# Two adjacency pieces loaded and widened during the expert slots, the ranks of a block taken three steps earlier, and no zero matmuls in front

## The chip, the cores and the metric

One Trainium2 chip, one core. The metric is the device time of one execution in microseconds (us), the median of several runs.

## The reference, cut to what matters

A two-layer graph network (each node averages the features of its neighbours over 100,000 edges), a layer norm, and then three layers in which every node's averaged state goes to two of eight experts. Weak experts are one matrix with a relu, strong ones two matrices with a relu between.

```python
def _sage_conv(x, src, dst, W_l, b_l, W_r):
    summed = jax.ops.segment_sum(x[src], dst, num_segments=N_NODES)
    cnt = jax.ops.segment_sum(jnp.ones((src.shape[0],), x.dtype), dst, num_segments=N_NODES)
    return (summed / jnp.maximum(cnt, 1.0)[:, None]) @ W_l + b_l + x @ W_r
...
h = x @ W_in + b_in
for l in range(3):
    agg = segment_sum(h[src], dst, num_segments=N) / deg
    logits = concatenate([h, agg], axis=-1) @ router_W[l] + router_b[l]
    vals, idx = top_k(logits, 2); gates = softmax(vals, axis=-1)
    weak = relu(einsum('nh,ehf->nef', agg, weak_W[l]) + weak_b[l])
    sh = relu(einsum('nh,ehf->nef', agg, strong_W1[l]) + strong_b1[l])
    strong = einsum('nef,efh->neh', sh, strong_W2[l]) + strong_b2[l]
    moe = einsum('ne,neh->nh', gate_dense, concatenate([weak, strong], axis=1))
    h = h + sigmoid(h @ conf_W[l] + conf_b[l]) * moe
return h @ W_out + b_out
```

There are 3125 nodes, padded to 25 tiles of 128; the state h has 256 columns, the inner layer of a strong expert 512.

## The kernel before, in words

Every engine has its own instruction stream, and the streams meet at semaphores; nothing reorders the work, so its order is the order of the code.

**Prelude.** TensorE first issues 110 zero matmuls (L1388). Then four chunks of key look-ups (chunk m: four passes of L1397 and 8 times L1399, then 8 times L1401), each behind the comparison that VectorE writes for it (L710). VectorE's tables follow from them, and then a long loop builds the adjacency matrix by one-hot matmuls (L1424 to L1431; VectorE's one-hots L754).

**Aggregation.** The adjacency is stored in DRAM as 25 pieces (NB = 5 blocks of destination nodes b, NK = 5 groups of source nodes k). A piece is 128x3200 bf16, 800 KB, and holds SK = 5 steps s of 128x640. Passes p = 0 to 2 (`gather`, L1484) multiply bf16 pieces. Beside the matmuls of a block, TensorE does small work of the block before at places (k, s): in pass 2 the turning and projection at PLACES, and `ranks` (L1549, L1551), which counts how many rows before each row chose the same expert, at (3, 4). `ranks` waits for the choice of the block before (VectorE L966, semaphore a_sel); VectorE's `positions` (L922) waits for `ranks`. After block 3 of pass 2, VectorE also fills the table of the first EARLY = 12 slots (`table_counts`, `table_experts`, `table_places`) before it goes on to block 4 (`block_of_nodes`, L813); TensorE waits for that block with L1455.

Passes p = 3 and 4 are the experts' aggregations (`aggregate`, L1571). The state is kept as two fp32r halves: ScalarE copies the high half (`high_half`, L1328) out of the loaded new states `h_new`, and VectorE subtracts to get the low half (`low_half`, L1110). This goes in eight units u of tiles (UNITS: 1, 1, 1, 2, 5, 5, 5, 5 tiles). Pieces come as bf16 into the three buffers of `ring3` (`expert_piece`, L504) and are widened to fp32r by ScalarE (`widen`, L1317), in turns into `wide_a` and `wide_b`. Block 0 waits for its widened piece (e_conv) and at each step s for the low half of that tile's unit (c_lo).

**Slots.** Each of passes 2, 3 and 4 ends with SLOTS = 32 slots of 256 rows of one expert. SyncE loads the rows of slot j (L530) into one of three buffers once slot j - 3 is finished. TensorE turns them (L1646), multiplies by the first weights (L1657, `slot_hidden`) and the second (L1668, `slot_output`); ScalarE copies the turned rows (L1338) and takes the relu of four parts (L1341); VectorE adds the bias and scales (L1103, L1105); GpSimd adds the rows into h_rows in DRAM by an indirect DMA (L659). In TensorE's stream `slot_turn(j + 1)`, `slot_output(j)`, `slot_hidden(j + 1)` follow each other.

**From slots to the next aggregation.** When the last indirect DMA has landed, SyncE loads the new states u = 0 to 7 (`new_states_in`, L537), with pieces 0, 1, 2 of block 0 behind u = 3, 4, 5. `ring3` and `wide_b` lie on the same memory as the slots' buffers; `wide_a` and the high and low halves don't. There are two such changeovers, p = 2 to 3 and p = 3 to 4.

## Time and profile before

| | us |
|---|---|
| median of 3 runs | 2048.9 (2045.55 to 2051.56) |
| the profiled execution | 2050.06 |
| its span, first to last instruction | 2048.1 |
| TensorE busy | 1787.7 (87%) |
| VectorE busy | 892.3 (44%) |
| ScalarE busy | 829.3 (40%) |
| GpSimd busy | 618.4 (30%) |

The mean granted TensorE clock is 0.898 of full speed. The page of the profile has six parts: busy time, the span in slices, the DMA queues, the chain of work that ended last, groups of instructions with the idle time before them, and the DMA issues. A timeline row gives the start in us, the busy time, engine, line, operation and tiles, the count of merged instructions and, in brackets, how long the engine was idle before it and what released it.

### The profile page before, as it was taken

To read this page: it belongs to the slowest core of one execution; us is meant where nothing else is said; L and a number is where in the kernel's file an instruction comes from. 1 tells how busy PE (TensorE), PEld (TensorE's weight loads), DVE (VectorE), ACT (ScalarE), POOL (GpSimd) and SP (SyncE) were. 2 spreads that over 40 slices of the span, in tenths; PEclk is the share of its full clock that TensorE was granted. 3 is DMA by queue.
4 is the path that set the end of the run, shared out by engine and by line. 5 is a ranking of instruction groups with operands and counts; after the bars stand their busy time and mean duration, and the time that the engine had idled before them with its cause. 6 is when DMAs were issued, how large, how long until landed. Compare 5 with 4: busy or idle time off the path is not lost.

```text
span 2048.1 us, 30902 instructions
## 1 busy us (share of the span) xinstructions
PE 1787.7 (87%) x9855; PEld 1380.5 (67%) x9858; DVE 892.3 (44%) x2593; ACT 829.3 (40%) x1388; POOL 618.4 (30%) x593
## 2 busy tenths in 40 slices
PE   9756666689999997999969998999969998999974
PEld 4545555455666664888858877888858877888864
DVE  6679999744344435433321113533321113533324
ACT  6256666534322222333336563333336563333321
POOL 1234444300000033544430231544430231544430
PEclk8766666599999998999989998999989998999986
DMA  6970000224567772444457551444457551444441
GB/s 143 340 265 0 0 0 0 85 98 162 205 195 235 260 280 100 87 75 73 72 116 271 188 188 43 90 74 74 72 125 260 188 188 43 90 74 74 72 116 51
DMA packets 162537, 259.55 MB, mean 127 GB/s; under 512 B 27776, under 2 KB 136043, under 8 KB 162424
## 3 DMA queue, kind: packets, MB, share of 16 engines
q1 hardware_dynamic: 125960, 206.09, 31.3%
q0 software_dynamic: 36464, 51.98, 14.5%
q8 instruction: 68, 1.11, 0.2%
q14 instruction: 45, 0.37, 0.1%
HBM read 149.08 MB, written 108.94 MB: 126 GB/s over the span
## 4 chain that ended last, share of the span: by engine, by line
PE 76%; DVE 12%; issue 5%; ACT 3%; DMA 2%; DVEq 1%; SPq 1%; POOL 0%; ACTq 0%; POOLq 0%
PE psum L1657 17%; PE psum L1668 16%; PE psum L1484 14%; PE psum L1571 13%; DVE arena L754 7%; PE psum L1623 2%; PE psum L1464 2%; PE psum L1646 2%; PE psum L1431 2%; PE psum L1399 2%; PE psum L1429 1%; PE psum L1690 1%; PE psum L1617 1%; ACT wide_b L1317 1%; ACT wide_a L1317 1%
## 5 line engine op out<-in xcount | busy, mean ns | idle before, releaser
L659 POOL DMA_INDIRECT h_rows<-arena,idx x192 | 313.7, 1634 | 420.1 <-DVE arena L1105 386.8
L1341 ACT ACTIVATE arena<-psum,b1c 128x256 f32<-128x256 f32 x384 | 182.2, 475 | 465.6 <-PE psum L1657 465.5
L1657 PE MATMUL psum<-arena 128*128 128x256 f32 x1536 | 360.2, 388 | 7.2 <-ACT arena L1338 7.2
L1668 PE MATMUL psum<-arena 128*128 x1536 | 347.4, 379 | 0.0
L1657 PEld LDWEIGHTS psum<-arena 128*128 128x128 f32 x1536 | 280.1, 192 | 72.0 <-ACT arena L1341 20.0
L1484 PE MATMUL psum<-arena 128*128 128x384 bf16 (+1 forms) x1875 | 318.2, 327 | 0.5 <-ACT arena L1233 0.2
L1668 PEld LDWEIGHTS psum<-arena 128*128 128x128 f32 x1536 | 284.6, 190 | 34.8
L754 DVE TENSOR_TENSOR arena<-arena 125x1200 bf16<-125x1200 bf16 (+1 forms) x300 | 282.0, 1006 | 23.6 <-PE psum L1431 23.0
L634 POOL DMA_INDIRECT xs_d<-arena,pos x150 | 146.6, 978 | 404.8 <-DVEq L936 362.7
L1484 PEld LDWEIGHTS psum<-arena 128*128 128x128 bf16 x1875 | 181.9, 98 | 126.6 <-ACT arena L1236 3.3
L1103 DVE TENSOR_TENSOR arena<-psum,arena 128x256 f32<-128x256 f32 x192 | 80.9, 421 | 381.9 <-PE psum L1668 380.8
L594 POOL TENSOR_TENSOR arena<-arena 128x100 bf16 x200 | 136.1, 680 | 248.4 <-ACT arena L1194 244.8
L1571 PE MATMUL psum<-halves,wide_b 128*128 128x512 f32 x625 | 161.3, 402 | 19.4 <-ACT wide_b L1317 18.4
L1571 PE MATMUL psum<-halves,wide_a 128*128 128x512 f32 x625 | 161.2, 402 | 17.9 <-ACT wide_a L1317 16.8
L1196 ACT CAST arena<-psum 128x800 f32 x200 | 165.6, 828 | 0.2 <-issue 0.2
L1571 PEld LDWEIGHTS psum<-halves,wide_b 128*128 128x128 f32 x625 | 114.2, 190 | 42.2 <-issue 21.0
L1571 PEld LDWEIGHTS psum<-halves,wide_a 128*128 128x128 f32 x625 | 114.2, 190 | 40.7 <-issue 19.4
L1431 PE MATMUL psum<-arena 125*128 125x100 bf16 x1200 | 139.6, 270 | 0.0
L1431 PEld LDWEIGHTS psum<-arena 125*128 125x128 bf16 x1200 | 122.7, 134 | 25.0
L1424 PE MATMUL psum<-arena 128*128 128x2 bf16 x200 | 37.4, 187 | 110.9 <-DVE arena L754 95.5
L1429 PE MATMUL psum<-arena 125*128 125x200 bf16 (+1 forms) x400 | 108.4, 368 | 0.0
L1424 PEld LDWEIGHTS psum<-arena 128*128 128x128 bf16 x200 | 21.6, 108 | 126.7 <-issue 81.2
(252 smaller groups left out, 1772.8 us busy)
## 6 DMA issues: line engine op xcount, KB each, us to landing
arena<-adj_d SPq DMA_DIRECT2D x50, 800.0 KB, 4.4
ring<-adj_d SPq DMA_DIRECT2D x50, 800.0 KB, 4.4
xs_d<-zrow SPq DMA_DIRECT2D x8, 3432.0 KB, 27.3
arena<-xs_d SPq DMA_DIRECT2D x96, 264.0 KB, 2.8
adj_d<-arena SPq DMA_DIRECT2D x25, 800.0 KB, 4.1
h_rows<-zrow SPq DMA_DIRECT2D x1, 8192.0 KB, 39.3
h_new<-h_rows SPq DMA_DIRECT2D x12, 640.0 KB, 8.3
arena<-h_rows SPq DMA_DIRECT2D x10, 640.0 KB, 6.3
```

Source lines behind the costliest of these rows:

```text
L594: pool.tensor_tensor(a, first_w[:, u % 8], a, ALU.add).then_inc(s_first, 1)
L634: pool.indirect_dma_start(xs_d, bass.IndirectOffsetOnAxis(ap=pos[:, b % 2, k, t:t + 1], axis=0), pay_of(p, b)[:, k, t], None).then_inc(a_s ...
L659: pool.indirect_dma_start(h_rows, bass.IndirectOffsetOnAxis(ap=idx[:, j % 2, h:h + 1], axis=0), ybuf[:, j % 2, h], None, compute_op=ALU.ad ...
L754: v.tensor_tensor(oh, every, keys.rearrange("p (n o z) -> p n o z", z=2, o=1).broadcast_to(shape), ALU.is_equal).then_inc(ready, 1)
L1196: act.copy(adj[:, bass.ds(off[u] + WC, G * WC)].rearrange("p (b n) -> p b n", b=2), banks[:, :, WC:WC + GA]).then_inc(s_wide, 1)
L1341: act.activation(hid[:, j % 2, f], psum[:, 5 + f % 2, 0:M], ACT.Relu, bias=b1c[:, bass.ds(at_b1[j % LOAD] + f, 1)]).then_inc(b_hidf, 1)
L1429: pe.matmul(bank[:, 0:cols], oh1[:, q, n, :, z % 2], ohe[:, q % 2, g, 0:cols, z], start=(z == 0), stop=False, skip_group_check=True)
L1431: mm = pe.matmul(bank[:, bass.ds(rel[(q % 2 * k + g) * (G - NST) + z - NST], WC)], oh1[:, q, n, :, z % 2], oh2[:, q, (g * (G - NST) + z - ...
L1484: return pe.matmul(psum[:, t, 0:width], ring[:, k, s, t * P:(t + 1) * P], features[p][:, k * SK + s, 0:width], start=(k == 0 and s == 0), ...
L1571: return pe.matmul(psum[:, t, :], adj32[piece_no(p, b, k) % 2][:, s, t * P:(t + 1) * P], halves[:, k * SK + s].rearrange("p k f -> p (k f) ...
L1657: mm = pe.matmul(psum[:, 5 + f % 2, 0:M], w1s[:, j % 2, f // 2, kt, f % 2 * P:(f % 2 + 1) * P], xsT[:, j % 2, kt], start=(kt == 0), stop=( ...
L1668: mm = pe.matmul(psum[:, h, 0:H], hid[:, j % 2, f, h * P:(h + 1) * P], w1f[:, bass.ds(at_w2 + f * H, H)], start=(f == 0), stop=(f == FT - 1))
```

## The change

- Pieces 0 and 1 of block 0 of the next pass get a buffer `early` of their own, on the memory of the last 6400 bf16 columns of `halves` (tiles 18 to 24). SyncE loads both at slot EARLY = 12, when the scatters that read `pay_b` are done.
- ScalarE widens piece 0 in five parts of 128x640, one behind the relus of each of slots 22 to 26. Piece 1 goes into `wide_b` in five parts between the high halves: two behind u = 2, one behind u = 3, two behind u = 4. TensorE waits for it part by part (e_second).
- Pieces 2, 3 and 4 of block 0 go through `ring3`: loaded behind u = 4, 5 and 6 of the new states. Piece 2 is widened behind u = 5; pieces 3 and 4 in the stream of block 0.
- `ranks` of pass 2 goes from (3, 4) to (3, 1).
- The 110 zero matmuls are gone.

```diff
+        early = carve([2, SK, BN], BF16)
...
+            def early_piece(p, k):
+                sp.dma_start(early[:, k].rearrange("p s n -> p (s n)"), adj_d[:, k]).then_inc(e_early[k], 16)
+
             def expert_piece(p, b, k):
-                m = piece_no(p, b, k)
-                if b == 0 and k == 0:
-                    for g in range(2):
-                        sp.wait_ge(b_sc[g], 32 * SLOTS // 2 * (p - 2))
-                if m > 2:
-                    sp.wait_ge(e_conv, m - 2)
-                sp.dma_start(ring3[:, m % 3].rearrange("p s n -> p (s n)"), adj_d[:, b * NK + k]).then_inc(e_in[m % 3], 16)
+                r = ring_no(p, b, k)
+                if b:
+                    sp.wait_ge(e_conv, piece_no(p, b, k) - 2)
+                sp.dma_start(ring3[:, r % 3].rearrange("p s n -> p (s n)"), adj_d[:, b * NK + k]).then_inc(e_in[r % 3], 16)
...
                         sp.wait_ge(b_tab, 2 * (p - 2) + 2)
+                        if p < 4:
+                            for k in range(2):
+                                early_piece(p + 1, k)
...
                     new_states_in(p, u)
-                    if 3 <= u < 6 and p < 4:
-                        expert_piece(p + 1, 0, u - 3)
+                    if 4 <= u < 7 and p < 4:
+                        expert_piece(p + 1, 0, u - 2)
...
+            def widen_early(p, k, s):
+                if s == 0:
+                    act.wait_ge(e_early[k], 16 * (p - 2))
+                ins = act.copy(adj32[k][:, s], early[:, k, s])
+                if s == SK - 1:
+                    ins.then_inc(e_conv, 1)
+                elif k:
+                    ins.then_inc(e_second, 1)
...
+                    if p < 4 and SLOTS - 2 * SK <= j < SLOTS - SK:
+                        widen_early(p + 1, 0, j - (SLOTS - 2 * SK))
...
+                        if u == 6:
+                            act.wait_ge(e_second, (SK - 1) * (p - 1))
+                            act.wait_ge(e_conv, piece_no(p + 1, 0, 1) + 1)
                         high_half(p, u)
-                        if u == 3 or u == 4:
-                            widen(p + 1, 0, u - 3)
+                        if u == 5:
+                            widen(p + 1, 0, 2)
+                        for s in {2: (0, 1), 3: (2,), 4: (3, 4)}.get(u, ()):
+                            widen_early(p + 1, 1, s)
...
-            for _ in range(110):
-                pe.matmul(psum[:, 7, :], zeros_b[:, :], ones_b[:, :], start=True, stop=True)
...
-                        if n > 3 * NB - 1 and (k, s) == (3, 4):
+                        if n > 3 * NB - 1 and (k, s) == (3, 1):
                             ranks(2, n - 3 * NB)
...
                         for s in range(SK):
+                            if b == 0 and k == 1 and s < SK - 1:
+                                pe.wait_ge(e_second, (SK - 1) * (p - 3) + s + 1)
+                            elif b == 0 and k == 1:
+                                pe.wait_ge(e_conv, piece_no(p, b, k) + 1)
```

The new lines stand 10 to 28 lines lower in the changed kernel, so the same instruction has another line number there. ScalarE at the changeover from pass 2 to pass 3, before (behind the last relu of the slots, L1341; L1328 are the high halves, L1317 the widenings; ring_51 is `ring3`):

```order
L1341 ACTIVATE arena<-psum,b1c 128x256
L1328 CAST halves<-h_new 128x256 x3
L1328 CAST halves<-h_new 128x2x256
L1317 CAST wide_a<-ring_51 128x3200
L1328 CAST halves<-h_new 128x5x256
L1317 CAST wide_b<-ring_51 128x3200
L1328 CAST halves<-h_new 128x5x256 x3
```

and of the change (L1359 is the relu, L1346 the high half, L1331 a part from `early`, which lies in the arena, L1326 a widening from `ring3`):

```order
L1359 ACTIVATE arena<-psum,b1c 128x256
L1346 CAST halves<-h_new 128x256 x3
L1331 CAST wide_b<-arena 128x640 x2
L1346 CAST halves<-h_new 128x2x256
L1331 CAST wide_b<-arena 128x640
L1346 CAST halves<-h_new 128x5x256
L1331 CAST wide_b<-arena 128x640 x2
L1346 CAST halves<-h_new 128x5x256
L1326 CAST wide_a<-ring_51 128x3200
L1346 CAST halves<-h_new 128x5x256 x2
```

The widening of piece 0 is gone from here, and that of piece 1 is cut in five.

SyncE's DMAs at the same place, before (L537 new states, L504 pieces):

```order
L537 DMA h_new<-h_rows 128x256 x3
L537 DMA h_new<-h_rows 128x512
L504 DMA ring_51<-adj_d 128x3200
L537 DMA h_new<-h_rows 128x1280
L504 DMA ring_51<-adj_d 128x3200
L537 DMA h_new<-h_rows 128x1280
L504 DMA ring_51<-adj_d 128x3200
L537 DMA h_new<-h_rows 128x1280 x2
L504 DMA ring_51<-adj_d 128x3200 x2
```

and of the change (L547, L511):

```order
L547 DMA h_new<-h_rows 128x256 x3
L547 DMA h_new<-h_rows 128x512
L547 DMA h_new<-h_rows 128x1280
L511 DMA ring_51<-adj_d 128x3200
L547 DMA h_new<-h_rows 128x1280
L511 DMA ring_51<-adj_d 128x3200
L547 DMA h_new<-h_rows 128x1280
L511 DMA ring_51<-adj_d 128x3200
L547 DMA h_new<-h_rows 128x1280
```

Two pieces fewer are loaded here, and the unit u = 4 stands where the first piece stood.

TensorE in the last quarter of block 4 of pass 2, before (L1484 the aggregation, L1549 the first matmul of the ranks, L1551 its last, L1455 the turning of block 4):

```order
L1484 MATMUL psum<-arena 128x384 x50
L1549 MATMUL psum<-sel,tri 128x48
...
L1551 MATMUL psum<-sel,ones_s 128x8
L1484 MATMUL psum<-arena 128x384 x25
L1455 MATMUL psum<-ident,arena 128x128 x4
```

and of the change (L1507, L1572, L1574, L1478):

```order
L1507 MATMUL psum<-arena 128x384 x35
L1572 MATMUL psum<-sel,tri 128x48
...
L1574 MATMUL psum<-sel,ones_s 128x8
L1507 MATMUL psum<-arena 128x384 x40
L1478 MATMUL psum<-ident,arena 128x128 x4
```

The ranks stand 15 matmuls sooner.

## Rows read from the trace of the kernel before

**Rows 1.** Page, parts 1 and 4: TensorE's busy time, the last chain by engine.

```profile
PE 1787.7 (87%) x9855; PEld 1380.5 (67%) x9858; DVE 892.3 (44%) x2593; ACT 829.3 (40%) x1388; POOL 618.4 (30%) x593
...
PE 76%; DVE 12%; issue 5%; ACT 3%; DMA 2%; DVEq 1%; SPq 1%; POOL 0%; ACTq 0%; POOLq 0%
```

**Rows 2.** Timeline of the changeover from pass 2 to pass 3.

```profile
1064.03 1.77 SPq L537 DMA_DIRECT2D h_new<-h_rows  x4
1065.89 0.38 SPq L504 DMA_DIRECT2D ring<-adj_d  x1
...
1066.60 1.31 DVE L1110 TENSOR_TENSOR halves<-h_new,halves 128x256 fp32r<-128x256 f32 x3 [8.35 <-ACT halves L1328]
...
1068.56 0.62 ACT L1328 CAST halves<-h_new 128x512 fp32r<-128x512 f32 x1 [1.10 <-DMA h_new<-h_rows]
...
1070.62 2.86 ACT L1317 CAST wide_a<-ring 128x3200 fp32r<-128x3200 bf16 x1 [1.44 <-DMA ring<-adj_d]
...
1073.72 7.37 PE L1571 MATMUL psum<-halves,wide_a 128*128 128x512 f32 x25 [16.79 <-ACT wide_a L1317]
...
1080.85 1.27 ACT L1328 CAST halves<-h_new 128x1280 fp32r<-128x1280 f32 x1 [0.32 <-DMA h_new<-h_rows]
1080.93 5.83 PE L1571 MATMUL psum<-halves,wide_b 128*128 128x512 f32 x25
```

**Rows 3.** Timeline of the changeover from pass 3 to pass 4.

```profile
1525.63 0.86 DVE L1110 TENSOR_TENSOR halves<-h_new,halves 128x256 fp32r<-128x256 f32 x2 [8.25 <-ACT halves L1328]
...
1534.42 7.42 PE L1571 MATMUL psum<-halves,wide_b 128*128 128x512 f32 x25 [18.35 <-ACT wide_b L1317]
```

**Rows 4.** Timeline of ScalarE between two slots of pass 2.

```profile
1046.21 0.47 ACT L1341 ACTIVATE arena<-psum,b1c 128x256 f32<-128x256 f32 x1 [0.39 <-PE psum L1657]
...
1046.58 0.58 ACT L1338 COPY arena<-psum 128x512 f32<-128x512 f32 x1
...
1050.96 0.47 ACT L1341 ACTIVATE arena<-psum,b1c 128x256 f32<-128x256 f32 x1 [3.80 <-PE psum L1657]
```

**Rows 5.** Groups by line: ScalarE's copies of 128x640 and 128x3200, mean ns.

```profile
L1317 ACT CAST wide_a<-ring 128x3200 fp32r<-128x3200 bf16 x25 | 71.6, 2864 | 49.7 <-PE psum L1571 48.3 <-DMA ring<-adj_d 1.4
...
L408 ACT COPY arena<-arena 128x640 bf16<-128x640 bf16 x45 | 29.0, 721 | 5.4 <-PE psum L1484 5.3
```

**Rows 6.** Page, part 6: count, KB each, us from issue to landing.

```profile
arena<-adj_d SPq DMA_DIRECT2D x50, 800.0 KB, 4.4
...
arena<-xs_d SPq DMA_DIRECT2D x96, 264.0 KB, 2.8
```

**Rows 7.** Timeline around the ranks of block 3 of pass 2.

```profile
782.54 8.30 PE L1484 MATMUL psum<-arena 128*128 128x384 bf16 x50
...
786.02 0.20 DVE L966 TENSOR_TENSOR sel<-arena 128x40 bf16<-128x40 f32 x1
...
791.09 0.20 DVE L922 TENSOR_TENSOR arena<-psum,nxt 128x40 f32<-128x40 f32 x1 [4.14 <-PE psum L1551]
...
803.29 1.09 PE L1455 MATMUL psum<-ident,arena 128*128 128x128 f32 x4 [8.21 <-DVEq L825]
```

**Rows 8.** Timeline of TensorE in the prelude.

```profile
2.15 25.32 PE L1388 MATMUL psum<-arena 128*128 128x512 bf16 x108 [2.15 <-POOL arena L577]
30.31 0.38 PE L1397 MATMUL psum<-arena 1*125 1x400 bf16 x1 [2.84 <-DVE arena L710]
...
44.74 0.59 PE L1397 MATMUL psum<-arena 1*125 1x400 bf16 x1
...
60.31 0.38 PE L1397 MATMUL psum<-arena 1*125 1x400 bf16 x1
...
76.01 1.52 PE L1401 MATMUL psum<-arena 100*125 100x400 bf16 x8
```

**Rows 9.** Windows of 2 us: span, busy by engine, granted clock, DMA share, GB/s.

```profile
32.00:34.00 2.00, 2.00 (x8) 1.25 (x7) 0.95 (x3) 2.00 (x1) 0.00 (x0) 0.58 0.42 3
...
58.00:60.00 2.00, 2.00 (x8) 1.41 (x7) 0.00 (x0) 0.00 (x0) 0.00 (x0) 0.59 1.09 341
```

More of the change, by code:

```diff
@@ L322, in build @@
         c_hi = sem("high_halves"); c_lo = sem("low_halves")
+        e_early = [sem(f"early_piece_in_{k}") for k in range(2)]; e_second = sem("second_piece_widened")
         e_in = [sem(f"expert_piece_in_{k}") for k in range(3)]
@@ L385, in piece_no, with ring_no @@
             return (p - 3) * NB * NK + b * NK + k
+        def ring_no(p, b, k):
+            return (p - 3) * (NB * NK - 2) + b * NK + k - 2
         def unit_of(t):
@@ L1308, in widen @@
             def widen(p, b, k):
-                m = piece_no(p, b, k)
-                act.wait_ge(e_in[m % 3], 16 * (m // 3 + 1))
-                if m > 1:
-                    n, last = divmod(m - 2, NK)
-                    if last < NK - 1:
-                        act.wait_ge(e_used, (NK - 1) * n + last + 1)
-                    else:
-                        act.wait_ge(a_sum, sums_before(NB + n + 1))
-                act.copy(adj32[m % 2][:, :, :], ring3[:, m % 3]).then_inc(e_conv, 1)
+                m, r = piece_no(p, b, k), ring_no(p, b, k)
+                act.wait_ge(e_in[r % 3], 16 * (r // 3 + 1))
+                n, last = divmod(m - 2, NK)
+                if last < NK - 1:
+                    act.wait_ge(e_used, (NK - 1) * n + last + 1)
+                else:
+                    act.wait_ge(a_sum, sums_before(NB + n + 1))
+                act.copy(adj32[(b * NK + k) % 2][:, :, :], ring3[:, r % 3]).then_inc(e_conv, 1)
+            def widen_early(p, k, s):
[6 more added lines that the diff above has]
+                    ins.then_inc(e_second, 1)
             def low_sums(p, b):
@@ L1360, in _ @@
                         else:
-                            for k in range(2, NK):
+                            for k in range(3, NK):
                                 widen(p, b, k)
```

10 lines of the change are left out of this document (6 added, 4 removed).

## The prediction

> **What bounds the kernel now.** I read the page first: TensorE is busy 87% of the span and carries 76% of the chain that ended last [rows 1]. So a saved microsecond counts where TensorE stands still and somebody else is late. The table of waits, longest first, then gives TensorE's long single waits, and only three of them are touched here: the two changeovers from the slots to the next aggregation [rows 2, 3] and the wait for block 4 of pass 2 [rows 7]. Last I read the prelude, where zero matmuls are taken out [rows 8, 9]. In each timeline the reader should look at the bracket behind TensorE's row: how long it was idle, and who ended that.
>
> In the first changeover TensorE was idle for 16.79 us, until ScalarE had widened piece 0. The order of events is: new states issued at 1064.03; piece 0 issued behind four of them at 1065.89; the first low halves at 1066.60; piece 0 landed only at 1070.62, and its widening took 2.86 us; TensorE at 1073.72 [rows 2]. The second one is alike, 18.35 us, with the first low halves at 1525.63 and TensorE at 1534.42 [rows 3]. So the wait that ends last there is the load and the widening of the piece, and the next behind it is the low half of the first tile.
>
> **Term 1, the changeovers: -14.5 us.** Piece 0 is ready before the slots end. What is late next is the low half of unit 0. In the first changeover three low halves take 1.31 us, 0.44 each, so the first is done at 1066.60 + 0.44 = 1067.04. TensorE followed the widening by 1073.72 - (1070.62 + 2.86) = 0.24 us, so it starts at 1067.28: 6.4 us sooner [rows 2]. In the second: 1525.63 + 0.86/2 + 0.24 = 1526.30 against 1534.42: 8.1 us [rows 3]. The loads of u = 0 to 3 and all before them keep their order, so nothing moves that start.
>
> The start alone is no gain if TensorE stalls behind it. Step by step, in the first changeover:
> - Piece 0 takes TensorE 7.37 us in five steps of 1.5, so step 3 comes at 1071.7. It wants the low half of u = 3. ScalarE now puts two parts of piece 1 ahead of that unit's high half. A copy of 128x640 takes 721 ns [rows 5] (bf16 to bf16, the nearest row; a fifth of the whole widening, 2864/5 = 573, is the lower bound, and I take 721). So the high half moves from 1068.56 [rows 2] to about 1069.5 and the low half ends near 1070.9. In time, with 0.8 us to spare.
> - Piece 1 is wanted at 1067.28 + 7.37 = 1074.65. Its last parts come behind the high half of u = 4, and this unit is now loaded where piece 0 stood. It is smaller (640 KB against 800), so it lands by 1070.6 [rows 2]. High half about 1.3 us and two parts 1.4 us: piece 1 is ready near 1073.5. The new memory for both pieces is written during the slots.
> - Piece 2 is wanted 5.83 us after piece 1 [rows 2], at 1080.5. Its buffer is free when piece 0 is used up, at 1074.65; with 2.86 us of widening it is ready near 1078.
> - Piece 3 is wanted at 1086.3, and may be widened from 1080.5 on. ScalarE has to take the high half of u = 7 first. Before, the last unit landed by 1080.85 [rows 2], behind seven units and three pieces; now it stands behind seven units and three pieces as well, so at the same time. Its high half ends at 1082.1 and piece 3 is ready at 1085.0, with 1.3 us to spare. This is the thinnest place; I take no wait, and keep 0 to 4 us per changeover (the widening and the high half both on the path) for the range.
>
> **Term 2, the restart: +1.0 us.** The first 25 matmuls after the idle time took 7.37 us and the next 25 took 5.83 [rows 2]: after the standstill TensorE runs at the lower of its two clock levels and rises within the first piece. This costs 1.5 us already. How soon the clock rises after an earlier start isn't shown. From zero (as before) to another 1.5 us each; I take 0.5 for each changeover.
>
> **Term 3, the slots: 0, cover named.** Five of the 32 slots of two passes get a ScalarE copy of 0.72 us behind the last relu. It delays the copy of the next turned rows, which starts at 1046.58 and takes 0.58; the first user is the relu at 1050.96, behind 3.80 us of idle time of ScalarE [rows 4]. 0.72 of 3.80 fits, and TensorE meanwhile has the 16 matmuls of `slot_output`. If the cover were gone, it would cost 10 x 0.72 = 7.2 us. The two early pieces are issued on SyncE's queue ahead of the rows of slot 12, but behind those of slot 11, so they have a whole slot, 7.4 us, before the rows of slot 12 are due to be issued; a piece takes 4.4 us to land, the rows 2.8 (medians) [rows 6]. If the loads overlap fully, those rows land some 4 us late, and they are needed a slot after their issue. Cost 0, at most 2 x 4.4 = 9 us.
>
> The GpSimd queue is touched only through the DMA engines: its indirect adds run on while 1.6 MB go by. The Trainium skill, page "DMA: Bandwidth & Descriptors", section "Queues, rings and completion order", says that each DMA engine takes turns between the queues that have work for it. By that rule a slot's add would land some us later once per pass; two slots may pass before VectorE's buffer is needed, so the sum would stay the same.
>
> **Term 4, the ranks: -2.5 us.** VectorE had nothing to do for 4.14 us until `ranks` came, at 791.09. From there it runs without a gap through positions, slot table and block 4, and TensorE waits 8.21 us for that, until 803.29 [rows 7]. The ranks now come 15 matmuls sooner: 15 x 8.30/50 = 2.5 us, at 788.2. The choice that they need is there at 786.02 + 0.20 [rows 7], 2 us before, so TensorE doesn't wait for it. VectorE's chain and TensorE's start move by the full 2.5. What is late next is TensorE's own aggregation, which ended 8.2 us sooner; there is room. The three other blocks of the pass have the same pattern with nobody waiting behind the ranks: 0.
>
> **Term 5, the zero matmuls: +1.8 us.** They end at 27.5, and VectorE's comparison lets the first real ones go only at 30.31 [rows 8]: none of the 25.3 us is on the path. What they leave is the clock. The granted clock falls within the window from 32 us and rises again within that from 58 us [rows 9]. At full clock a chunk takes (77.53 - 60.31)/2 = 8.6 us; the second, nearly all at half clock, took 15.57, and with its last 0.7 us at half clock 16.2; the first took 14.43, as it began at full clock [rows 8]. Without the zero matmuls the first is at half clock too: 16.2 - 14.4 = +1.8 us, all on TensorE's path, since it has no idle time between chunks. Floor: the clock may rise at the end of the first chunk instead of the second: 15.6 + 3 x 8.6 = 41.4 against 47.2 before, -5.8. Ceiling: a chunk later, 2 x 16.2 + 15.6 + 8.6 = 56.6, +9.4.
>
> The Trainium skill, page "TensorE: Matmul & The Clock Gate", section "Why this matters for your kernels", advises to warm TensorE up first and warns that a pause gives the clock back. Its first half speaks against this edit, its second says that the warm-up was largely wasted, as the 2.8 us pause stood behind it; rows 8 and 9 show both, and the sum goes by them.
>
> **Sum.** -14.5 + 1.0 + 0 - 2.5 + 1.8 = -14.2 us on the profiled execution, 2050.06 to 2035.9. The median of before is 2048.9, 1.2 us under that execution, so I forecast 2048.9 - 14.2 = **2034.7 us**. Nothing between these places waits for a transfer with a fixed date, so savings pass on to the end.
>
> **Rivals.**
> - *The clock rises a chunk sooner in the prelude* (-5.8 instead of +1.8): 2027.1. For it: the last matmuls of the first chunk are of the same kind as those in which it rose. Against: it did not rise there before. 0.17.
> - *It rises a chunk later* (+9.4): 2042.3. 0.08.
> - *Pieces 2 to 4 or the parts of piece 1 come late*, and TensorE stands still again 3 to 4 us in each changeover: 2034.7 + 7 = about 2042. For it: five parts on ScalarE in a chain where everything waits for everything. Against: the step list above. 0.15.
> - *The slots are lengthened* by the copies or by the 1.6 MB ahead of slot 12: +7.2 to +9, 2042 to 2044. Against it: 3.80 us of idle time [rows 4]. 0.06.
> - *The changeovers do not shorten*, since the low half isn't the next but something not seen, such as the memory of piece 1: 2034.7 + 14.5 - 1 = 2048.2, no difference. 0.03.
> - *Slower*: without the zero matmuls the clock stays at half level through all four chunks of the prelude: 4 x 16.2 = 64.8 against 47.2, +17.6 in place of +1.8: 2050.5. It decides from the point where the prelude loses over 1.8 + 14.2 = 16.0 us, and loses more than 0.3% only if the one-hot loop behind it slows as well. Against: the clock rose in matmuls that stay. 0.02.
>
> The forecast itself has 0.49. The range: 2027.1 stands at the lower end and 2042 to 2043 at the upper, so **2027 to 2043**; it leaves out the two last rivals and a tail at each side. A difference of under 0.3%, 6.1 us, can't be told from none with this kernel. So faster is everything under 2042.8: 0.91; within 0.3%: 0.07; slower: 0.02.
>
> **What the profile of the changed kernel would show.** TensorE's wait at each changeover about 10.3 us, ended by VectorE's low half, not by ScalarE's widening; no second wait of over 1 us in the two pieces behind it. Slots 22 to 26 as long as the others, 7.4 us. The wait for block 4 down from 8.2 to about 5.8. No L1388, the first chunk of the prelude 16.2 us, and the end of the last chunk at 79.3. What would make the prediction wrong: another place of the rise in the prelude; a wait of TensorE for piece 2 or 3; VectorE's chain behind the ranks held by another wait.

## The result, and the profile after

The changed kernel takes 2038.7 us, the median of 5 runs (2032.5 to 2041.0), against 2048.9 us before, also of 5 runs (2045.6 to 2056.2). The ratio is 0.9948 (0.9931 to 0.9965): 10.2 us or 0.5% faster. The forecast was 2034.7 us, a gain of 14.2. The profiled execution took 2040.89 us with a span of 2039.1, so it stands 9.2 us below the profiled execution of before. The same kernel, run again later beside its own runs of before, gave 2035.0 us against 2047.4, ratio 0.9936 (0.9916 to 0.9957). Ratios leave out runs that lie over 1.5% above the fastest run of the same kernel, while medians in us hold all runs; this matters only for the second group of experiments below.

The page gives TensorE 15.7 us less busy time than [rows 1], in 108 fewer matmul records, which are the zero matmuls (25.3 us); the rest of TensorE's work is longer by some 10 us, at the lower clock. TensorE's share of the last chain is the same. Part 1 and part 4 of the page of after:

```profile
PE 1772.0 (87%) x9747; PEld 1376.1 (67%) x9748; DVE 892.9 (44%) x2593; ACT 829.7 (41%) x1404; POOL 619.0 (30%) x593
...
PE 76%; DVE 12%; issue 5%; ACT 3%; DMA 2%; DVEq 1%; SPq 1%; POOL 0%; ACTq 0%; POOLq 0%
```

**The changeovers.** The table of TensorE's waits of after (waiter and releaser, us in total, times, longest) has both of them in one row, ended by VectorE's low half:

```profile
PE psum L1594 <- DVE halves L1120: 20.4, 2, 10.2
```

The timeline of the first one (start, duration, engine and line, tiles, count, idle time before and who ended it) answers to [rows 2]; its last row is the start of the second, which answers to [rows 3]:

```profile
1068.76 8.71 PE L1594 MATMUL psum<-halves,wide_a 128*128 128x512 f32 x25 [10.18 <-DVE halves L1120]
1077.31 5.83 PE L1594 MATMUL psum<-halves,wide_b 128*128 128x512 f32 x25
...
1088.64 5.83 PE L1594 MATMUL psum<-halves,wide_b 128*128 128x512 f32 x25
...
1072.91 1.35 ACT L1331 CAST wide_b<-arena 128x640 fp32r<-128x640 bf16 x2
...
1077.56 2.87 ACT L1326 CAST wide_a<-ring 128x3200 fp32r<-128x3200 bf16 x1 [0.44 <-PE psum L1594]
...
1082.94 1.26 ACT L1346 CAST halves<-h_new 128x1280 fp32r<-128x1280 f32 x1 [1.35 <-DMA h_new<-h_rows]
1084.11 2.87 ACT L1326 CAST wide_b<-ring 128x3200 fp32r<-128x3200 bf16 x1
...
1522.81 8.68 PE L1594 MATMUL psum<-halves,wide_a 128*128 128x512 f32 x25 [10.19 <-DVE halves L1120]
```

The waits fell from 16.79 to 10.18 us and from 18.35 to 10.19. Behind the start TensorE has no gap. Piece 3, the thinnest place, was ready at 1084.11 + 2.87 = 1086.98 and wanted at 1088.64, so 1.7 us were left where 1.3 had been worked out. Most of that margin came from the slow first piece: with 7.37 us in place of 8.71, piece 3 would have been wanted 1.3 us sooner. In e2_early_only, whose first piece took 7.52 us at the second changeover, TensorE did wait 0.48 us for piece 3. But the first 25 matmuls now take 8.71 and 8.68 us, where they took 7.37 and 7.42. The granted clock says why. Windows of 2 us from the new start (span, busy time by engine, granted clock, DMA share, GB/s) stay at 0.50, the lower level of 1.2 GHz, until the fourth:

```profile
1072.00:1074.00 2.00, 2.00 (x6) 1.54 (x5) 0.96 (x1) 2.00 (x3) 0.00 (x0) 0.50 0.98 408
1074.00:1076.00 2.00, 2.00 (x9) 1.64 (x8) 0.53 (x1) 0.41 (x2) 0.00 (x0) 0.82 1.04 431
```

**The ranks.** The timeline answers to [rows 7]: the wait for block 4 fell from 8.21 to 5.78 us.

```profile
793.20 0.19 PE L1572 MATMUL psum<-sel,tri 128*128 128x48 bf16 x1
...
805.82 0.45 PE L1478 MATMUL psum<-ident,arena 128*128 128x128 f32 x1 [5.78 <-DVEq L835]
```

**The prelude.** The timeline of TensorE answers to [rows 8], with the start of each of the four chunks, the same eight matmuls ahead of the rise and behind it, and the last matmuls:

```profile
30.80 0.56 PE L1420 MATMUL psum<-arena 1*125 1x400 bf16 x1 [30.80 <-DVE arena L720]
...
46.95 0.59 PE L1420 MATMUL psum<-arena 1*125 1x400 bf16 x1
47.47 2.93 PE L1422 MATMUL psum<-arena 100*125 100x400 bf16 x8
...
63.12 0.59 PE L1420 MATMUL psum<-arena 1*125 1x400 bf16 x1
...
76.49 2.27 PE L1424 MATMUL psum<-arena 100*125 100x400 bf16 x8
78.69 0.38 PE L1420 MATMUL psum<-arena 1*125 1x400 bf16 x1
79.00 1.57 PE L1422 MATMUL psum<-arena 100*125 100x400 bf16 x8
...
85.82 1.52 PE L1424 MATMUL psum<-arena 100*125 100x400 bf16 x8
```

The first two chunks take 16.2 us each, and the third 15.6: the clock rose only at its end, near 78 us, a chunk later than before. The prelude ends at 87.3 us where it ended at 77.5.

Here the level has to be read from the durations (eight equal matmuls take 2.93 us or 1.57 us). A window of after, in the form of [rows 9], shows a granted clock of 1.00 in the middle of the slow stretch:

```profile
60.00:62.00 2.00, 2.00 (x8) 1.38 (x7) 0.00 (x0) 0.00 (x0) 0.00 (x0) 1.00 1.08 340
```

The column reads 1.00 through the slow part of the prelude in every execution without matmuls ahead of it. So the mean granted clock of such a kernel (0.907 for after) is too high, and can't be held against the 0.898 of before.

Putting the profiled executions side by side at five places (us; the end of the prelude, the end of the one-hot loop at VectorE's first lay-out copy, TensorE's start on block 4 of pass 2, its start on pass 3 and on pass 4):

| | prelude | loop | block 4 | pass 3 | pass 4 | span |
|---|---|---|---|---|---|---|
| before | 77.5 | 393.3 | 803.3 | 1073.7 | 1534.4 | 2048.1 |
| after | 87.3 | 399.9 | 805.8 | 1068.8 | 1522.8 | 2039.1 |
| difference | +9.8 | +6.6 | +2.5 | -5.0 | -11.6 | -9.0 |

The pieces of that -9.0 are: waits at the changeovers -14.8, restart +2.6 (1.34 and 1.26), ranks -2.4, prelude +9.8, and -3.2 that the one-hot loop gives back. Another -1.4 is one stretch near 462 to 472 us in which before had a granted clock of 0.83 and after 1.00. That makes -9.4, and +0.4 is left over.

### The profile page after: what moved, and what is told of

Read it like the earlier page. It is cut to its first block, busy times and chain, and to the rows that moved or that the text cites. A ratio compares the mean times of both kernels' runs of the same rounds, so it can differ in the third digit from the quotient of the medians.

```text
span 2039.1 us, 30707 instructions
## 1 busy us (share of the span) xinstructions
PE 1772.0 (87%) x9747; PEld 1376.1 (67%) x9748; DVE 892.9 (44%) x2593; ACT 829.7 (41%) x1404; POOL 619.0 (30%) x593
## 3 DMA queue, kind: packets, MB, share of 16 engines
q0 software_dynamic: 36464, 51.98, 14.5%
## 4 chain that ended last, share of the span: by engine, by line
PE 76%; DVE 12%; issue 5%; ACT 3%; DMA 2%; DVEq 1%; SPq 1%; POOL 0%; ACTq 0%; POOLq 0%
PE psum L1685 17%; PE psum L1696 16%; PE psum L1507 14%; PE psum L1594 13%; DVE arena L764 7%; PE psum L1651 2%; PE psum L1487 2%; PE psum L1674 2%; PE psum L1422 2%; PE psum L1454 2%; PE psum L1452 1%; PE psum L1645 1%; PE psum L1718 1%; DVEq L764 1%; PE psum L1478 1%
## 5 line engine op out<-in xcount | busy, mean ns | idle before, releaser
L1359 ACT ACTIVATE arena<-psum,b1c 128x256 f32<-128x256 f32 x384 | 181.8, 473 | 462.5 <-PE psum L1685 462.5
L1507 PE MATMUL psum<-arena 128*128 128x384 bf16 (+1 forms) x1875 | 316.9, 326 | 0.5 <-ACT arena L1243 0.2
L1507 PEld LDWEIGHTS psum<-arena 128*128 128x128 bf16 x1875 | 181.5, 98 | 125.7 <-ACT arena L1246 3.2
L1594 PE MATMUL psum<-halves,wide_a 128*128 128x512 f32 x650 | 171.3, 409 | 21.5 <-DVE halves L1120 20.4
L1594 PE MATMUL psum<-halves,wide_b 128*128 128x512 f32 x600 | 153.8, 400 | 1.1 <-issue 1.1
L1594 PEld LDWEIGHTS psum<-halves,wide_a 128*128 128x128 f32 x650 | 121.8, 195 | 46.6 <-issue 23.4
L1594 PEld LDWEIGHTS psum<-halves,wide_b 128*128 128x128 f32 x600 | 108.5, 188 | 22.1 <-issue 2.2
```

What stands on the lines that cost most here:

```text
L1359: act.activation(hid[:, j % 2, f], psum[:, 5 + f % 2, 0:M], ACT.Relu, bias=b1c[:, bass.ds(at_b1[j % LOAD] + f, 1)]).then_inc(b_hidf, 1)
L1507: return pe.matmul(psum[:, t, 0:width], ring[:, k, s, t * P:(t + 1) * P], features[p][:, k * SK + s, 0:width], start=(k == 0 and s == 0), ...
L1594: return pe.matmul(psum[:, t, :], adj32[(b * NK + k) % 2][:, s, t * P:(t + 1) * P], halves[:, k * SK + s].rearrange("p k f -> p (k f)"), s ...
```

## The experiments

Three theories were to be told apart. **A:** the early pieces bring 14 us or more, and the clock of the prelude is a matter of chance that the zero matmuls don't decide. **B:** the zero matmuls were of use, and taking them out costs the missing 4 us (or the 9.8 us of the profile). **C:** the copies and loads among the slots cost something that the changeovers' gain hides. The experiments ran in three groups, and each group had its own chip and its own runs of before. The chip of the second group is slower as a whole; the last section comes back to it.

**The parts, one at a time**

e1_zeros_back is the changed kernel with the zero matmuls back:

```diff
@@ tensor, ahead of the prelude
             pe.wait_ge(s_const, 4)
+            for _ in range(110):
+                pe.matmul(psum[:, 7, :], zeros_b[:, :], ones_b[:, :], start=True, stop=True)
```

> The changed kernel with the 110 zero matmuls back in front. Theory A (the zero matmuls only keep the first 2 us of the prelude at full clock; in which chunk the clock rises is chance): the first chunk is 1.8 us shorter than in the changed kernel, the median 1 to 2 us lower, 2037, and the chunk of the rise differs from run to run in both. Theory B (without the zero matmuls the clock rises a chunk later as a rule): the prelude's last look-up matmul ends near 77.5 us instead of 87.3, and the median is 5 to 7 us lower, about 2033.

e2_early_only also puts the ranks back, so only the early pieces are left of the change:

```diff
-                        if n > 3 * NB - 1 and (k, s) == (3, 1):
+                        if n > 3 * NB - 1 and (k, s) == (3, 4):
```

> Kernel before with the early pieces alone (zero matmuls kept, ranks at (3, 4)). Theory: both changeovers shrink as in the changed kernel, 6.6 and 8.2 us to TensorE's first matmul, less 1.3 us each because the clock stays low longer behind it: 12.2 us together, 2036.7. The slots keep their 7.4 us. Rival (the copies of ScalarE or the loads at slot 12 lengthen the slots): under 10 us gained, with slots 12 to 14 or 22 to 26 longer.

e3_ranks_only is the kernel before with only that line changed the other way:

```diff
-                        if n > 3 * NB - 1 and (k, s) == (3, 4):
+                        if n > 3 * NB - 1 and (k, s) == (3, 1):
```

> Kernel before with the ranks at (3, 1) alone. Theory: TensorE's wait for block 4 of pass 2 goes from 8.2 to 5.7 us, and the slots begin 2.5 to 3 us sooner; about 2046. Rival (VectorE's chain is held by another wait): wait stays over 7 us, no difference.

e4_no_zeros_only is the kernel before without the 110 zero matmuls:

```diff
-            for _ in range(110):
-                pe.matmul(psum[:, 7, :], zeros_b[:, :], ones_b[:, :], start=True, stop=True)
```

> Kernel before without the zero matmuls, nothing else. Theory A: first chunk of the prelude 16.2 us instead of 14.4, median 1 to 2 us higher, about 2050.5. Theory B (the clock rises a chunk later as a rule): prelude ends 9 to 10 us later, of which some 3 come back in the one-hot loop behind it; about 2055.

Against 2049.1 us for before (23 runs), in the same group:

| | median us (runs) | ratio, interval | prelude ends | changeover waits |
|---|---|---|---|---|
| e1_zeros_back | 2033.1 (6) | 0.9934, 0.9911 to 0.9956 | 70.0 | 10.14, 10.06 |
| e2_early_only | 2035.1 (6) | 0.9930, 0.9914 to 0.9947 | 71.0 | 10.20, 10.06 |
| e3_ranks_only | 2047.9 (12) | 0.9997, 0.9981 to 1.0013 | 79.2 | 17.22, 17.33 |
| e4_no_zeros_only | 2047.4 (12) | 0.9990, 0.9975 to 1.0005 | 79.7 | 16.82, 16.91 |

The early pieces alone bring 14 us, at least what the whole change brings, so they are the change. The ranks alone cut their wait to the same length as in the changed kernel, as the timeline of e3_ranks_only shows:

```profile
787.59 0.19 PE L1549 MATMUL psum<-sel,tri 128*128 128x48 bf16 x1
...
800.21 1.09 PE L1455 MATMUL psum<-ident,arena 128*128 128x128 f32 x4 [5.78 <-DVEq L825]
```

In the time of the whole kernel those 2.4 us can't be told from nothing. Taking the zero matmuls out alone costs nothing that can be measured: 1.7 us less, with 5 us less and 1 us more as ends. That speaks against B, which expected 2055 us. Theory A had expected 1 to 2 us more, and that isn't seen either. Its 12 runs lie in groups, at 2043 to 2044, 2046 to 2049 and 2052 to 2055 us, as they might if the rise fell into one chunk or another; the one with a trace (2052.2 us) is of the slowest group, with the rise in the second chunk. The timelines show the rise itself. In e4_no_zeros_only it comes near 61 us, in the second chunk, as in before. In e1_zeros_back, which has the zero matmuls, it comes within the first:

```profile
30.76 0.38 PE L1422 MATMUL psum<-arena 1*125 1x400 bf16 x1 [2.92 <-DVE arena L720]
...
39.45 2.93 PE L1424 MATMUL psum<-arena 100*125 100x400 bf16 x8
42.17 2.09 PE L1426 MATMUL psum<-arena 100*125 100x400 bf16 x8
44.19 0.38 PE L1422 MATMUL psum<-arena 1*125 1x400 bf16 x1
```

Over all profiled executions, the chunk in which the clock rose was:

| | first | second | third |
|---|---|---|---|
| with 110 zero matmuls (before, e1, e2, e3) | 2 | 2 | 0 |
| without (after, e4, e7, e8, e9, e12, e13) | 3 | 3 | 1 |

So neither kernel fixes it. The changed kernel, unaltered, ended its prelude at 87.3, 73.7 and 79.1 us (after, e9, e13), with the rise in the third, first and second chunk. In every one of these executions TensorE is busy without a gap through the chunks at the lower level, and once the clock rises the rest of the prelude is at the upper one. In all eleven the rise falls within the last eight matmuls of a chunk, those of the ones matrix (L1401 of before), which then take 2.0 to 2.7 us where they take 2.87 at the lower level and 1.52 at the upper. So the rise isn't free to come anywhere; what is special there, and what picks the chunk, is not shown.

**Clock kept up: a bridge and fillers**

e5_zeros_bridge lets the zero matmuls last until the prelude's first real one, with no pause:

```diff
             pe.wait_ge(s_const, 4)
+            for _ in range(126):
+                pe.matmul(psum[:, 7, :], zeros_b[:, :], ones_b[:, :], start=True, stop=True)
```

> The changed kernel with 126 zero matmuls in front, 16 more than before had, so that they last until the first comparison is ready (about 30.9 us) and TensorE has no pause ahead of the look-ups. If the pause is what took the clock away, the whole prelude stays at full clock: four chunks of 8.6 us, last look-up at 65.5 us instead of 87.3 in the changed kernel (70 to 71 with 110 zero matmuls in two runs with an early rise), median 2028 to 2032. If the look-up matmuls themselves don't keep the clock, it falls within the first chunk all the same and the time is that with 110, about 2033.

The clock never fell. The chunks took 8.6 us each, and the prelude ended at 66.4 us. The 16 extra matmuls were a few too many, and held up the first real one to 32.0 us, about 1 us. The time was 2119.5 us (12 runs), ratio 0.9960 (0.9921 to 0.9999), against 2128.9 for before and 2125.0 for e9_changed_again, the changed kernel as it is on that chip, with ratio 0.9968. From these two ratios no gain of the bridge can be told.

e8_fillers puts matmuls of the identity into the wait at each changeover:

```diff
                     pe.wait_ge(b_yt, 2 * SLOTS * (p - 2))
+                    for _ in range(72):
+                        pe.matmul(psum[:, 3, 0:P], ident[:, :], ident[:, :], start=True, stop=True)
```

> The changed kernel with 72 matmuls of the identity with itself in each of the two changeovers, into a bank nobody reads, while TensorE waits for the first low half. They last about 8 of its 10.2 us. If the low clock is what makes the first piece slow (8.7 us for 25 matmuls against 5.8), the first piece takes 5.8 and each changeover gains 2.9 us, 5.8 together, about 2033 against the changed kernel. Rival: the fillers hold up the first real matmul, or the first piece is slow because of its waits for low halves step by step; no gain or a loss of some us.

The edit was mis-sized. A matmul of fp32 by fp32 has two records of 0.11 us each, so 72 of them are 144 records and last 16.3 us, past the low half that was being waited for. Timeline of e8_fillers:

```profile
1059.89 16.32 PE L1604 MATMUL psum<-ident 128*128 128x128 f32 x144 [1.08 <-DVE arena L1113]
1075.96 5.95 PE L1594 MATMUL psum<-halves,wide_a 128*128 128x512 f32 x25
```

The start came some 6 us too late. Its time, 2128.9 us (6 runs, 2096.9 to 2139.4; ratio 0.9894, 0.9801 to 0.9987), is spread too widely to say anything. The second row does: the first 25 matmuls took 5.95 us and not 8.6. So the whole slow restart is the clock, and it goes when TensorE is kept busy. How much it costs without fillers doesn't follow the length of the wait. The first 25 matmuls behind each changeover, first and second, took (us): with the long waits of before 7.37 and 7.42 (before), 7.29 and 7.36 (e4), but 8.43 and 8.29 (e3); with waits of 10 us 8.71 and 8.68 (after), 8.70 and 8.74 (e1), 8.70 and 8.64 (e13), 8.57 and 8.39 (e9), 8.20 and 8.69 (e7), but 7.28 and 7.52 (e2), 7.31 and 7.55 (e12), and 7.26 and 8.29 (e5). In e5 it differs within one execution, between two waits of 10.1 us. The unaltered changed kernel, though, has 8.4 to 8.7 in all six places of its three traces, so how far it is chance stays open.

> The changed kernel once more, unaltered, beside the others. If the chunk of the prelude in which the clock rises is chance, this run's prelude may end anywhere from 71 to 88 us, and the median lies between the two seen so far for kernels with all three other edits, 2033 and 2039. If the missing zero matmuls make it late as a rule, the prelude ends at 87 again and the median is 2038 to 2039.

This run was there to stand beside e5 and e8. It gave 2125.0 us (12 runs), ratio 0.9968 (0.9922 to 1.0013): on this chip the gain can't be told from none. Its prelude ended at 73.7 us, with the rise in the first chunk, which again speaks against B.

e10_bridge_fillers puts both together in the right sizes: 121 zero matmuls, and 36 fillers at each changeover.

```diff
+            for _ in range(121):
+                pe.matmul(psum[:, 7, :], zeros_b[:, :], ones_b[:, :], start=True, stop=True)
...
+                    for _ in range(36):
+                        pe.matmul(psum[:, 3, 0:P], ident[:, :], ident[:, :], start=True, stop=True)
```

> The changed kernel with 121 zero matmuls in front (they end about 1 us sooner than the 126, which held the first look-up up to 32.0 us) and 36 matmuls of the identity in each changeover (the 72 came out as 144 records of 0.11 us and lasted 16.3 us, too long; 36 last 8.1 us, inside the 10.2 us wait). Theory: the prelude ends at 65.4 us instead of 71 to 88, and of that difference two thirds are left behind the one-hot loop; each first piece takes 5.9 us instead of 8.5, so 5 to 6 us more. Together 9 to 15 us under the changed kernel on the same chip. Rival: TensorE kept busy loses the clock elsewhere (the one-hot loop, the aggregation), and what is gained here is lost there.

It takes 2025.3 us (5 runs, 2024.1 to 2026.5), ratio 0.9890 (0.9871 to 0.9910). The changed kernel in the same group, e13_changed_third, takes 2035.0 (6 runs), so the two edits bring 9.7 us more, at the low end of the 9 to 15 expected. Timeline of TensorE in e10_bridge_fillers, the start of the prelude and the first changeover:

```profile
2.15 29.02 PE L1413 MATMUL psum<-arena 128*128 128x512 bf16 x119 [2.15 <-POOL arena L587]
31.11 0.38 PE L1422 MATMUL psum<-arena 1*125 1x400 bf16 x1
31.41 1.57 PE L1424 MATMUL psum<-arena 100*125 100x400 bf16 x8
...
1047.30 8.28 PE L1606 MATMUL psum<-ident 128*128 128x128 f32 x72 [1.07 <-DVE arena L1113]
1057.37 5.93 PE L1596 MATMUL psum<-halves,wide_a 128*128 128x512 f32 x25 [1.79 <-DVE halves L1120]
...
1075.74 5.96 PE L1596 MATMUL psum<-halves,wide_b 128*128 128x512 f32 x25 [0.94 <-ACT wide_b L1326]
```

The prelude ends at 65.5 us, and the first piece is 2.8 us shorter than in e13. At the second changeover two low halves come late for the faster TensorE, by 0.2 and 0.8 us. TensorE now reaches piece 3 before it is ready and waits 0.94 us for ScalarE: the thinnest place of the prediction's list is the one that binds once the restart is gone. The runs also lie closer together, 2.5 us from the first to the last where the changed kernel's lie 10.5 us apart. That is what one expects if the spread is for the most part the place of the clock's rise. The Trainium skill, page "TensorE: Matmul & The Clock Gate", section "Why this matters for your kernels", warns that a pause between bursts of matmuls gives the clock back; the bridge and the fillers agree with it.

e11_all goes one step further. It moves the ranks to (2, 4), and puts 16 fillers into the wait for block 4:

```diff
-                        if n > 3 * NB - 1 and (k, s) == (3, 1):
+                        if n > 3 * NB - 1 and (k, s) == (2, 4):
...
+                    pe.wait_ge(n_taken, unit(4 * NB - 1, 0))
+                    for _ in range(16):
+                        pe.matmul(psum[:, 7, 0:P], ident[:, :], ident[:, :], start=True, stop=True)
```

> As the run with 121 zero matmuls and 36 fillers, and the ranks of pass 2 ten matmuls sooner still, at (2, 4), with 16 fillers in TensorE's wait for block 4 of pass 2. The choice that the ranks need is ready 2 us before them in the changed kernel, so 1.6 us of 10 matmuls fit: wait for block 4 from 5.8 to 4.1 us, and with the clock kept the projection and the first slot lose some 3 us of slow matmuls. 3 to 5 us under the run without these two. Rival: TensorE waits for the choice, or the fillers hold the turning of block 4 up: no gain.

It takes 2021.4 us (4 runs, 2019.1 to 2025.5), ratio 0.9868 (0.9846 to 0.9891), whose interval overlaps that of e10. Block 4 starts at 792.55 where it starts at 793.02 in e10, but TensorE was 1.2 us behind e10 from 413 us on, long before the ranks. Counted from the last product ahead of the ranks (774.18 in e10, 775.34 in e11), block 4 comes 1.6 us sooner, which is what ten matmuls last. VectorE was still idle for 1.70 us ahead of `positions` in e10 and isn't idle there in e11, so a further step of the ranks would bring nothing. The clock fell shortly behind block 4 all the same (0.66 granted from 800 to 810 us, as in e10).

**The slots**

e7_parts_bunched puts all five parts of piece 0 behind one slot instead of one part behind each of five:

```diff
-                    if p < 4 and SLOTS - 2 * SK <= j < SLOTS - SK:
-                        widen_early(p + 1, 0, j - (SLOTS - 2 * SK))
+                    if p < 4 and j == SLOTS - SK - 1:
+                        for s in range(SK):
+                            widen_early(p + 1, 0, s)
```

> The changed kernel with all five parts of piece 0 widened behind one slot, 26, instead of behind five. The cover is ScalarE's 3.80 us of idle time between the copy of the turned rows and the next relu. Five parts take 3.4 us and come ahead of that copy, which ends some 4 us later than now; the weights' first matmul of the next slot wants it about 3.1 us after its usual start. So slot 27 begins about 1 us late and nothing else changes. If the cover is larger than I read it, TensorE has no wait at all there; if ScalarE's copies disturb TensorE in another way, slot 26 is longer by more than 2 us.

It was run once, for its trace, on the slow chip (2130.7 us, which says nothing by itself). The timeline of ScalarE and TensorE around that slot:

```profile
1026.69 3.22 ACT L1331 CAST wide_a<-arena 128x640 fp32r<-128x640 bf16 x5
1029.81 0.58 ACT L1356 COPY arena<-psum 128x512 f32<-128x512 f32 x1
...
1030.45 3.79 PE L1686 MATMUL psum<-arena 128*128 128x256 f32 x16 [0.37 <-ACT arena L1356]
```

Five parts take 3.22 us, and only then does TensorE wait, for 0.37 us. So the start of slot 27 is late by about half of the 1 us expected, the cover is about 2.9 us, and one part of 0.72 us is well inside it. C falls for the copies. In the changed kernel itself the idle time of ScalarE shrinks from 3.80 us [rows 4] to 3.18 and the slot stays at 7.4 us (985.44 to 992.85):

```profile
985.44 0.47 ACT L1359 ACTIVATE arena<-psum,b1c 128x256 f32<-128x256 f32 x1 [3.80 <-PE psum L1685]
...
988.47 0.72 ACT L1331 CAST wide_a<-arena 128x640 fp32r<-128x640 bf16 x1
...
992.85 0.47 ACT L1359 ACTIVATE arena<-psum,b1c 128x256 f32<-128x256 f32 x1 [3.18 <-PE psum L1685]
```

The 1.6 MB at slot 12 do delay somebody. GpSimd's indirect adds wait for a transfer, for two slots, and have caught up by the third. TensorE's slots stay 7.4 us apart. The same place in after, queue of SyncE and GpSimd:

```profile
889.33 0.88 SPq L505 DMA_DIRECT2D arena<-adj_d  x2
...
898.36 1.55 POOL L669 DMA_INDIRECT h_rows<-arena,idx  x1 [6.05 <-DMA h_rows<-arena,idx]
...
904.32 1.55 POOL L669 DMA_INDIRECT h_rows<-arena,idx  x1 [2.55 <-DMA h_rows<-arena,idx]
...
910.94 1.69 POOL L669 DMA_INDIRECT h_rows<-arena,idx  x1 [3.21 <-DVE arena L1115]
```

**The one-hot loop**

The prelude lost 9.8 us, but the loop behind it ended only 6.6 us later. Other executions show the same: with the prelude's end at 65.5 us the loop takes 319.6 us (e10), at 70.0 us 317.5 (e1), at 77.5 us 315.7 (before), at 87.3 us 312.5 (after). About a third of what the prelude saves is lost again. What ends at a fixed time there are the fills with zeros that SyncE issues at the start: in before, after, e1, e10 and e13 the last of them is over at 139 to 141 us, wherever the prelude ended. e12_short_fill is the changed kernel without the last of them, 8192 KB of spare rows of `h_rows`. They only take the adds of empty places, and nothing reads them:

```diff
-            sp.dma_start(h_rows[P * S:P * S + SLOTS * M].rearrange("(p r) f -> p r f", p=P),
-                         zrow[:, 0:H].unsqueeze(1).broadcast_to((P, SLOTS * M // P, H))).then_inc(s_zx, 16)
...
-            pool.wait_ge(s_zx, 16 * (NE + 1))
+            pool.wait_ge(s_zx, 16 * NE)
```

> The changed kernel without the zero fill of the last 8192 spare rows of h_rows (8192 KB; nothing reads these rows, they take what the empty places of a slot add). It asks why a third of what the prelude loses comes back in the one-hot loop. Theory: the loop's turns are slower while the zero fills of DRAM run (VectorE idle 2 to 4 us a turn until about 140 us, 0.3 to 0.5 after), so a loop that begins later meets less of them. Then a fill that ends some 24 us sooner makes the loop 3 to 5 us shorter at the same start, and the median some 4 us lower. Rival: the slow turns belong to the first turns of the loop, whatever the fills do; loop and time unchanged.

> The changed kernel unaltered, as the measure for the three beside it. Theory: prelude end anywhere from 71 to 88 us, the two changeover waits 10.2 us, the wait for block 4 5.8 us, and 8 to 12 us under the kernel before.

e12_short_fill takes 2022.7 us (5 runs, 2021.1 to 2027.5), ratio 0.9882 (0.9861 to 0.9903), 12.4 us less than the 2035.0 of e13_changed_third. The loop takes 306.3 us instead of 315.0, behind a prelude that ended 1.4 us later. That is more than the 3 to 5 us expected, and less than in any execution with the fill named above. Windows of both, 125 to 136 us, first e13 and then e12:

```profile
125.00:136.00 11.00, 4.79 (x44) 3.69 (x41) 6.55 (x8) 4.75 (x11) 2.99 (x5) 0.66 1.09 387
```

```profile
125.00:136.00 11.00, 6.98 (x68) 5.50 (x65) 10.52 (x12) 6.99 (x15) 4.82 (x8) 0.66 0.00 0
```

While the fill runs at 387 GB/s, TensorE does 44 matmuls where it does 68 without it, at the same granted clock. These windows hold a single long stop of e13; in the 6 us from 119 us on, ahead of it, it is 30 against 42, and in the 6 us from 132 us on, behind it, 36 against 36. A matmul or copy takes no longer for it; the engines stand still between them. The longest stop, in e13:

```profile
126.04 0.83 ACT L1208 CAST arena<-psum 128x800 f32 x1
...
131.85 0.18 PE L1449 MATMUL psum<-arena 128*128 128x2 bf16 x1 [6.08 <-issue]
...
134.07 3.80 DVE L766 TENSOR_TENSOR arena<-arena 125x1200 bf16<-125x1200 bf16 x4 [4.45 <-PE psum L1456]
```

TensorE stood for 6.08 us and the profile shows nothing that it waited for, while VectorE and ScalarE waited for TensorE. Each of the 13 profiled executions with the fill has one to three such stops, of 3.7 to 6.4 us, all of them ending between 104 and 142 us; e12 has none. "Issue" would fit an instruction stream that arrives late because its own transfers (the page lists 1.10 MB on a DMA queue of kind instruction) go through the busy DMA engines. No run tests that, so the cause within the loop stays open; that the fill causes it is shown. Not all of the 12.4 us is the loop's: in the profiled pair 8.7 us is the loop, and 2.5 us is the first pieces behind the two changeovers (7.31 and 7.55 against 8.70 and 8.64), which the fill doesn't explain.

## Why the prediction was right, and where it was off

- **Term 1 (-14.5 us) was right**: -6.6 and -8.2 in the profile where -6.4 and -8.1 had been worked out. The rival that pieces come late fell, and so did the one that the changeovers don't shorten. The first of these was closer than the sum made it: most of piece 3's margin came from the slow restart, and with a faster one TensorE waited 0.48 us (e2) and 0.94 us (e10) for it. The method that worked was to ask at each changeover which event stood second, and then to check the next four deadlines.
- **Term 2 (+1.0 us) was undersized.** It measured +2.6 in the profiled execution, near its upper bound of 3.0, where "I take 0.5 for each" had been chosen. The step that was off is to take before's 7.37 us as a norm and to add a little for the earlier start. The earlier start is not the reason: e3 with the long waits of before has 8.43 and 8.29 us, and e2 and e12 with the short ones have 7.3 to 7.6. Over all traces it is 7.3 to 8.7 us with either wait, and what sets it is not shown. The size of the whole restart is 1.4 to 2.9 us per changeover against the 5.83 to 5.93 us at full clock.
- **Term 3 (0) was right**, with its cover: 0.6 of 3.80 us were used, and e7 shows that TensorE waits only when about 2.9 us are used up. The loads ahead of slot 12 touched the indirect adds for two slots and nobody on the path.
- **Term 4 (-2.5 us) was right** in the profile (-2.4 in after and in e3), and it is too small to be seen in the medians.
- **Term 5 (+1.8 us)** had the right length of a chunk at the lower level (16.2 us), but it treated the chunk of the rise as a property of the kernel, with before as the norm. The tables show that it differs from one execution to the next in either kernel. The 14.4 us of the first chunk weren't fixed either: with the same zero matmuls and the same chunk of the rise, e3 took 16.0. The profiled execution was the rival "a chunk later": +9.8 where +9.4 had been worked out. In the medians, e4 puts the term between -5 and +1 us, which leaves +1.8 just outside.
- **"Savings pass on to the end" failed** for the prelude. The one-hot loop takes back about a third of what the prelude gains and gives back a third of what it loses, since the fill behind it ends at its own time.

The forecast of 14.2 us is 4.0 above the 10.2 measured and 1.8 above the 12.4 of the later group. The interval of the measured ratio is some 3.5 us wide on either side, so the forecast lies just outside it in the first group and inside it in the later one. In the profiled pair the difference of 5.0 us is restart 1.6 and prelude 8.0 too much, against 3.2 from the loop and 1.4 from the stretch near 462 us, which weren't foreseen. So terms that were 9.6 us too low were half made up for by two effects that the prediction hadn't seen, and that is luck. For the medians the same split isn't shown, since only one execution of each kernel per group has a trace; the largest term in it, the prelude, differs by execution. The range of 2027 to 2043 held the time, on the slower side of the forecast.

## What to carry to other kernels

When a wait is taken away, the time goes only down to the event that stood second, and that one can be read in the timeline of before; the next few deadlines behind it can be listed and checked in the same way. Where TensorE stands still for some 10 us, a part of the price is paid after the wait, as matmuls at half clock. Cheap matmuls that end just before the real ones took away 2.8 us per changeover and, in the prelude, 22 us against the worst profiled execution (65.5 against 87.3) and 4.5 against the best (70.0), of which the next stage took a third back. And transfers that nobody waits for, such as a fill with zeros, have a price as well if they run beside a dense loop: 8.7 us in the loop here.

## What the runs showed of the hardware that was not expected

**Busy is not the same as warm.** In the prelude TensorE is busy 2.00 us of every 2.00 and still stays at 1.2 GHz for a long time: in e1 from about 33 to 43 us by the granted clock, in after from 31 to 78 us by the durations. These are matmuls on 100 of the 128 rows. With the bridge of e10 every one of them took its time of 2.4 GHz, and the four chunks took 34.4 us where after needed 56.5. In the four executions with 110 zero matmuls, a pause of 1.9 to 2.9 us behind them was followed by the lower clock within 2.5 us of the first real matmul.

**On one chip the clock falls in the middle of the aggregations.** The second group ran on a chip on which before takes 2128.9 us instead of 2047 to 2049. In block 2, 3 and 4 of pass 3 of e9 its granted clock falls to half for about 24 us each and comes back, and TensorE is busy throughout these stretches. Windows of pass 3, first in e9_changed_again and then in e13_changed_third, the same program on another chip:

```profile
1160.00:1180.00 20.00, 20.00 (x65) 17.10 (x65) 2.89 (x26) 4.52 (x4) 0.00 (x0) 0.50 0.23 69
```

```profile
1160.00:1180.00 20.00, 19.04 (x98) 15.18 (x97) 3.59 (x14) 13.34 (x15) 9.03 (x10) 1.00 0.56 185
```

Each of the three stretches follows a standstill of TensorE of 1.9 us, at the start of the second piece of the block, which lasts 0.27 us on the other chip. The first in e9, and the same place in e13:

```profile
1156.47 2.29 PE L1595 MATMUL psum<-halves,wide_b 128*128 128x512 f32 x5 [1.89 <-issue]
...
1143.72 1.39 PE L1596 MATMUL psum<-halves,wide_b 128*128 128x512 f32 x5 [0.27 <-issue]
```

A standstill of that length isn't always followed by a fall: in e5, on the same chip, one of 1.86 us ended at 1150.91 and the granted clock stayed at 1.00. Why TensorE stands still for longer on this chip isn't shown.

The executions of before there spread over 42 us, so differences of 10 us between medians of that group carry little, and the verdicts above on e5, e8 and e9 rest on their timelines.
